# One kernel, one change: which engine makes the rounded part of a split weight tile

## The reference

```
mod = silu(c) @ w_mod                       # six vectors of 512
h   = layernorm(x) * (1 + ca) + sa
# Mamba-2 block: 128 heads of 64 channels, state 128, 8 groups, chunks of 128 tokens
proj = h @ in_proj.T -> gate (8192), hBC (8192 + 2*8*128), dt (128)
hBC  = silu(causal conv over 4 tokens (hBC));  xs, B, C = split(hBC)
dt   = clip(softplus(dt + bias));  decay from cumsum(dt * A)
Y    = (C B^T * decay) (xs dt)  +  C * state carried from chunk to chunk  +  D * xs
g    = Y * silu(gate);  out = g * rsqrt(mean over its group (g^2)) * norm_w
x    = x + ga * (out @ out_proj.T)
x    = x + gb * ((layernorm(x) * (1 + cb) + sb) @ sign(w_ffn).T + bias)
```

## Time and profile before

| what | value |
|---|---|
| device time, median of 3 runs | 1877.42 us (1868.88 to 1879.78) |
| the profiled execution's own time | 1870.32 us |
| its span (first to last instruction) | 1868.5 us |
| busy: PE, DVE, ACT, POOL | 1754.7, 1290.5, 1065.5, 942.1 us |
| mean granted TensorE clock | 0.988 of full speed |

### The profile page before, as it was taken

The page is one execution under the profiler, slowest core; times in us unless marked ns, Lnnn a source line. Parts: engine busy times, 40 slices in busy tenths (PEclk is TensorE's granted clock), DMA queues, the critical chain, the costliest instruction groups (busy, mean ns, idle before and its releaser), DMA issues.

```text
span 1868.5 us, 31134 instructions
## 1 busy us (share of the span) xinstructions
PE 1754.7 (94%) x9656; PEld 1344.0 (72%) x9656; DVE 1290.5 (69%) x2095; ACT 1065.5 (57%) x1946; POOL 942.1 (50%) x721
## 2 busy tenths in 40 slices
PE   6799999999999999999999999999999999999966
PEld 5567777777777777777777777777777777777755
DVE  5766667666766677766676667666777666766788
ACT  6566555656646565665546566465656555565632
POOL 2355453556535464554535555355644545455563
PEclk9899999999999999999999999999999999999988
DMA  6412121111202121121211212121211212111121
GB/s 224 130 30 69 55 66 44 50 60 57 66 28 72 49 66 51 35 66 55 66 45 48 62 54 68 29 72 45 70 51 29 72 55 66 44 48 61 34 96 57
DMA packets 77097, 114.14 MB, mean 61 GB/s; under 512 B 21376, under 2 KB 28032, under 8 KB 76032
## 3 DMA queue, kind: packets, MB, share of 16 engines
q1 hardware_dynamic: 59360, 80.06, 14.2%
q10 hardware_dynamic: 17568, 31.99, 5.1%
HBM read 88.94 MB, written 23.07 MB: 60 GB/s over the span
## 4 chain that ended last, share of the span: by engine, by line
issue 46%; POOL 34%; PE 9%; DVE 5%; ACT 3%; DMA 1%; SPq 1%; POOLq 1%; ACTq 0%; DVEq 0%
POOL yt L1605 9%; POOL ssq L1600 7%; POOL wg_lo L1524 4%; POOL wo_lo L1524 4%; POOL prev L1586 3%; POOL yt L1608 3%; POOL wx_lo L1524 3%; PE bank L476 2%; PE bank L478 2%; PE bank L477 2%; PE bank L641 1%; PE bank L706 1%; DMA raw_w<-w_in_dram 1%; PE bank L840 1%; ACT lm L1072 0%
## 5 line engine op out<-in xcount | busy, mean ns | idle before, releaser
L1605 POOL TENSOR_TENSOR yt<-yt,ea 128x384 f32<-128x384 f32 (+1 forms) x128 | 189.6, 1481 | 393.1 <-DVE ea L1440 393.1
L1218 DVE SCALAR_TENSOR_TENSOR xc<-bank,bpar,xc 128x511 f32<-128x511 f32 (+2 forms) x384 | 285.4, 743 | 52.8 <-ACT xc L906 48.3
L1410 DVE TENSOR_TENSOR lm<-lm,cbm 128x512 f32<-128x512 f32 x256 | 185.9, 767 | 155.7 <-ACT lm L1075 155.7
L476 PE MATMUL bank<-h_hi,wg_hi 128*128 128x512 f32 x640 | 262.0, 409 | 31.3 <-ACT gate L1030 21.9
L478 PE MATMUL bank<-h_hi,wg_lo 128*128 128x512 f32 x640 | 251.0, 392 | 0.0
L477 PE MATMUL bank<-h_lo,wg_hi 128*128 128x512 f32 x640 | 250.2, 391 | 0.0
L476 PE MATMUL bank<-wo_hi,g_hi 128*128 128x512 f32 x496 | 206.9, 417 | 7.2 <-POOL wo_lo L1524 7.2
L476 PE MATMUL bank<-h_hi,wx_hi 128*128 128x512 f32 x512 | 210.3, 411 | 2.2 <-DVE bt L1218 2.2
L1586 POOL TENSOR_TENSOR prev<-prev,dec 128x512 f32<-128x512 f32 x96 | 102.0, 1063 | 206.0 <-DVE prev L1356 131.9
L478 PE MATMUL bank<-h_hi,wx_lo 128*128 128x512 f32 x512 | 200.3, 391 | 0.0
L477 PE MATMUL bank<-h_lo,wx_hi 128*128 128x512 f32 x512 | 199.9, 390 | 0.0
(11 more groups left out here) (187 smaller groups left out, 3796.9 us busy)
## 6 DMA issues: line engine op xcount, KB each, us to landing
raw_w<-w_in_dram SPq DMA_DIRECT2D x145, 256.0 KB, 2.6
raw_w<-w_out_dram SPq DMA_DIRECT2D x64, 256.0 KB, 2.6
part_d<-part ACTq DMA_DIRECT2D x64, 256.0 KB, 2.0
part<-part_d ACTq DMA_DIRECT2D x58, 256.0 KB, 2.7
rt<-rows_d SPq DMA_DIRECT2D x256, 8.0 KB
acc<-x_dram SPq DMA_DIRECT2D x8, 256.0 KB, 6.6
acc<-w_mod_dram SPq DMA_DIRECT2D x2, 1024.0 KB, 6.0
lh<-neg_d SPq DMA_DIRECT2D x128, 8.0 KB
```

What stands on the lines that cost most here:

```text
L476: nc.tensor.matmul(out_ap, whi(k), hhi(k), start=(k == 0), stop=False)
L1218: stt(dst[:, at], ps[:, 0:HALF - 3 + k], w(k), dst[:, at], ALU.mult, ALU.add)\
L1410: tt(lm[:, h % 4, :], lm[:, h % 4, :], cbm[:, toks(hf)], ALU.mult).then_inc(v_m, 1)
L1605: tt(yt[:, j % 2, cols], yt[:, j % 2, cols], ea[:, j % 2, cols], ALU.add).then_inc(p_t3, 1)
```

## The change

For the 198 tiles filled within the units (26 in each of seven groups and 16 in the last), POOL makes `hi` itself with a `tensor_copy`, waits for that copy to complete, and then makes `lo` as before. ACT does nothing for these tiles. POOL now waits itself for the matmuls that free the old tile (`ge(po, s, value)`) and for the landing of the load (`d_w`); it also counts up a semaphore `p_take` on which nothing waits. The places of the fills in POOL's list stay. The 11 tiles of the prologue are made as before, `hi` on ACT.

```
--- before.py
+++ after.py
+        p_hi, p_take = sem("p_hi"), sem("p_take")
...
 # ACT
-            def unit_fill(f, g):
-                kind, j, _, k, s, value = f
-                ge(se, s, value)
-                split_fill(kind, j, (FILLS0 + k) % 2, (FILLS0 + k) // 2 + 1 + FILLS // 2 * g)
...
-                todo = by_step(fills(g, c, 0, last))
                 for z in range(1, NZ):
                     silu_gate(u, c, z)
...
-                    if z < 3:
-                        for f in (todo[0] if z == 1 else []) + todo[z]:
-                            unit_fill(f, g)
-                late = todo[3]
...
                 exp_a(0)
                 decays(0)
-                for f in late:
-                    unit_fill(f, g)
...
                         tap(item, item_bank(n), nv, hv, g + 1, pv)
                         n += 1
-                    for f in todo[j:j + 1]:
-                        if first and j == 0:
-                            se.wait_ge(d_scr, 16 * 14)
-                        unit_fill(f, g)
...
 # POOL
             def unit_fill(f, g):
-                kind, j, _, k, _, _ = f
-                lower(kind, j, (FILLS0 + k) % 2, FILLS0 + FILLS * g + k + 1)
+                kind, j, _, k, s, value = f
+                hi, lo = W_SLOTS[kind]
+                raw = raw_w[:, (FILLS0 + k) % 2, :]
+                ge(po, s, value)
+                po.wait_ge(d_w[(FILLS0 + k) % 2], 16 * ((FILLS0 + k) // 2 + 1 + FILLS // 2 * g))
+                po.sem_inc(p_take, 1)
+                nc.gpsimd.tensor_copy(hi[:, j, :], raw).then_inc(p_hi, 1)
+                po.wait_ge(p_hi, FILLS * g + k + 1)
+                tt(lo[:, j, :], raw, hi[:, j, :].bitcast(F), ALU.subtract).then_inc(p_w, 1)
...
                     for f in todo[j:j + 1]:
+                        if first and j == 0:
+                            po.wait_ge(d_scr, 16 * 14)
                         unit_fill(f, g)
```

More of the change, by code:

```diff
@@ L1063, in unit @@
                 pv = (c // 2) if hf == 0 else (c // 2 + 1) % 2
-                todo = fills(g, c, 1, last)
                 def decays(j):
```

## The result

The changed kernel takes 1918.57 us in the median (1916.16 to 1920.73, 4 runs), the kernel before on the same chip 1873.15 (1868.12 to 1879.78, 4 runs). The ratio is 1.0249, with a 95% interval of 1.0229 to 1.0269: 45 us slower. The forecast was 1905, in a range of 1881 to 1931; 32 us were forecast and 45 came. The profiled execution took 1917.80 us, 47.5 more than the one before.

What follows compares the result with a forecast made beforehand. POOL's stretch without idle time at the end of even units was taken to bind; 24.0 + 6.0 - 4.2 + 6.4 = +32 us on 1870.3 gave 1902.5, put at 1905 for the median, range 1881 to 1931.

Steps and rivals of the forecast that it cites:

- What bounds: For the last 11 us of each even unit POOL, half idle in the mean, binds; PE waits at its end.
- The price of a copy: Each POOL fill: copy 0.67 us plus 0.08 us wait for completion, C = 0.75 us, between 0.61 and 1.38.
- rival B: POOL's copy costs like a subtraction, or its waits and count cost that much: C = 1.38, +52 to +62 us; chance 0.15.
- Even to odd: End of even units: the last two wo copies delay PE's out projection by 2C, 16 times: +24.0 us.
- `c` = 1 to `c` = 2: POOL's add for the last `j` comes C later, delaying `silu` and PE's transposes, eight times: +6.0 us.
- Collisions behind `j` = 1: POOL's subtractions, shifted by the copies, meet DVE's L1410 pairs differently: 8 x (0.7 + 0.7 - 0.6) = +6.4 us.
- ACT without fills: In `c` = 3, ACT's gate, table load and `ea` come earlier, shortening PE's seven waits for `acc`: 7 x -0.6 = -4.2 us.
- The signs: Copy near 0.67 us; longer `wo_lo` waits; L706 waits about 1 us; smaller `acc` waits; POOL busy 1075 us, ACT 940.
- signs of being wrong: Copy over 1 us, wait for `wo_lo` not growing, or PE waiting in a place where it did not before.

Runs made afterwards that it cites:

- The spare copy: Kernel before, plus a POOL copy nothing uses ahead of the subtraction of each even unit's last two wo fills (32 copies): 1896.66 us, ratio 1.0136.
- the kernels by place: Kernel before, POOL making `hi` in one place only: first phases 1876.84 us, even units 1908.93, odd units' second phase 1881.06.
- the two fillers: Changed kernel with unused matmuls inside PE's waits: six at each odd head, 1912.66 us; nine more inside the wait for `acc`, 1903.18 us.

## Why the prediction was right, and where its sizes were off

**What bounds.** Right: POOL's stretch without idle time at the end of the even units, half idle as POOL is. The spare copy shows it with nothing else changed, and the kernels by place show that the same copies cost little elsewhere.

**The price of a copy.** I took 0.67 us between 0.53 and 1.30. The rows after (ns min/median/max) say 0.62 in the median, and 1.1 where DVE is in the way:

```profile
L1517 POOL CAST wo_hi<-raw_w x64: 601/620/1096, 114.0 to 1810.1; 128x512 fp32r<-128x512 f32 x64
```

The mean of the 64 is 0.79, that of all 198 is 0.76. The self-wait is 0.08 as taken (1028.01 + 0.61 to 1028.70). The copy was nearer to the memset than to the subtraction, rival B is out. The other waits and the count cannot be seen in this stretch.

**Even to odd.** Forecast +24.0 at 16 heads, with PE's wait at 0.45 + 1.5 each. Measured: the out projection there comes 18.7 us later against the matmuls ahead of it (25.9 less 7.2, and the pairing too), 1.2 each. The last copy and the subtraction behind it share one collision with `g_lo`, where the subtraction alone had it before, and the add between the fills got shorter, 1.00 in place of 1.48. So the two copies lengthen the stretch by 1.20 us, not 1.5. The transposes ahead of it now wait for `silu` too, 0.4 us each, which I had named for `c` = 1 only; in the 15 even units between the heads that adds 8.2 us, and the shorter waits for the gate in front of them give 7.9 back.

**`c` = 1 to `c` = 2.** Forecast +6.0 for the silu, and 5.6 of the collisions belong to this unit too. Measured: 10.3 us by the pairing, without the clock's part, and +8 to +11 with the odd units' copies alone. Right in its place and a little small. What I hadn't asked is who waits for the fill ahead of that add. PE does, eight times, 5.5 us, at matmuls where it waited some 0.2 us for the gate before:

```profile
1084.37 0.49 PE L477 MATMUL bank<-h_hi,wg_hi 128*128 128x512 f32 x1 [0.83 <-POOL wg_lo L1519]
...
1088.27 0.65 PE L707 MATMUL bank<-ident,xc 128*128 128x128 f32 x4 [0.91 <-ACT xc L1013]
```

It is the fill of `j` = 2, whose copy collided and took 1.14 us; the gate projection needs it. This wait isn't a further cost: 4 us later, and in all eight units, PE waits again, for `silu` ahead of the transposes, and that wait sets when they start.

**Collisions behind `j` = 1.** Forecast +0.7, +0.7 and -0.6 us for the pairs of L1410. The rows that answer to the earlier trace rows are 2.22 and 2.23 us in place of 1.55, the one of the earlier trace rows 1.96 in place of 2.65: +0.67, +0.68 and -0.69. Right, and in the even units it reaches PE in full: its waits for the convolution behind that pair are 4.7 us longer in seven units `c` = 0 and 5.6 shorter in eight `c` = 2. The pair in `c` = 0:

```profile
1020.60 2.22 DVE L1394 TENSOR_TENSOR lm<-lm,cbm 128x512 f32<-128x512 f32 x2 [0.31 <-ACT lm L1065]
```

**ACT without fills.** This step failed: "7 x -0.6 = -4.2 us", measured +3.8 at those matmuls. ACT did what I said. It waits for PE's `ea` now, not for a load:

```profile
1157.03 0.60 ACT L1070 ACTIVATE ea<-bank 128x512 f32<-128x512 f32 x1 [3.32 <-PE bank L670]
```

But POOL's four fills with copies fall beside DVE's work of that place:

```profile
1156.38 1.82 DVE L1310 SCALAR_TENSOR_TENSOR acc<-part,rstd,acc 128x512 f32<-128x512 f32 x1
...
1161.84 1.73 DVE L1310 SCALAR_TENSOR_TENSOR acc<-part,rstd,acc 128x512 f32<-128x512 f32 x1
```

The operation that PE waits for takes 1.73 us, and the pair ahead of it 2.05. In the kernel before they are

```profile
1130.40 1.29 DVE L1410 TENSOR_TENSOR lm<-lm,cbm 128x512 f32<-128x512 f32 x2 [1.52 <-ACT lm L1075]
...
1132.33 1.04 DVE L1326 SCALAR_TENSOR_TENSOR acc<-part,rstd,acc 128x512 f32<-128x512 f32 x1
```

I had looked at collisions behind `j` = 1 alone. That the x fills account for about half of the first phase's part is measured; that it is this collision is read from the trace.

**The clock.** Not in the sum at all, and the largest gap: 18.8 us by the pairing, of which 15.2 between the first and the last head, and 15 by the two fillers. In the trace before the clock was full in the whole middle, and I did not ask what PE's waits, grown from 0.5 to 1.6 and from 1.6 to 2.1 us, would do to it.

**The signs.** The copy, the waits for `wo_lo` and the eight at L706 (0.9 us each) came as said. The waits on `acc` did not get smaller. One of the signs of being wrong came: PE waits in a place where it did not wait before, ahead of the transposes at the 16 odd heads. The busy times missed: POOL 1064 us where I said 1075, ACT 965 where I said 940. A rounding took 0.63 us, but the instruction behind it started 0.54 us after it, so each frees less than its length.

**The sum.** What each place got longer between the first and the last head, by the pairing and without the clock's part:

| place | forecast, us | measured, us |
|---|---|---|
| even to odd, the wait for `wo_lo` | +24.0 | +18.7 |
| `c` = 1 to `c` = 2, with its collisions | +6.0 + 5.6 | +10.3 |
| collisions in `c` = 0 | +5.6 | +4.7 |
| collisions in `c` = 2 | -4.8 | -5.6 |
| ACT without fills, the wait for `acc` | -4.2 | +3.8 |
| sum | +32 | +32 |

(The +18.7 takes in the first head itself.) The same sum is luck: a term that was 5 us too high and some smaller ones stand against one that had the wrong sign and was 8 us too low. The clock comes on top, with nothing in the forecast against it, and the range was wide enough for both. Rival B's lower end was added up wrongly, too: 1870.3 + 52 is 1922, not 1925, which changes nothing here.

## What to carry to other kernels

An engine that is half idle can still be the one that binds, for a stretch: look in its timeline for where the idle time before its instructions stops, and whether the busiest engine starts right behind the end. Work moved onto it costs most there (the other two places together took 12 to 17 us, by kernels of their own), and the same work one place earlier, where it idles, may even win (here the plain move of a fill gained 16 us, while the move from engine to engine lost 45). Here waits of PE of 1.6 to 2.4 us cost up to twice their length, since the clock fell behind them; compare the granted clock of both kernels before you price such a wait. And ask of an engine that you load more which operations of its neighbour it will then meet.

## What was not expected of the hardware

- Waits of 1.6 and 2.3 us in an otherwise busy PE were followed by stretches at half clock in some passes of the loop and not in others (ten such stretches in the middle of the changed kernel's trace, seven behind the head of a unit `c` = 1 and three behind the wait for `acc`). In the execution before, seven waits for `acc` of up to 1.9 us had none behind them. Matmuls that nothing uses, put into the waits, kept it full and were worth 15 us.
- A copy on POOL with one input took 0.60 to 0.68 us in 138 of 198 cases. The other 60 took 1.00 to 1.16, and each of them began while DVE was at an operation with two inputs in SBUF; so a one-input copy is held up like a two-input one.
